# One decoder layer on one core: attention score products from float32r parts on two row halves, and a new order of the products

## The reference

```python
q = (x @ w_q.T).reshape(B, S, 16, 16); k = ...; v = ...
scores = jnp.einsum('bqhd,bkhd->bhqk', q, k) * scale      # 4 x 16 heads, each 1024 x 1024
weights = jax.nn.softmax(scores, axis=-1)
out = jnp.einsum('bhqk,bkhd->bqhd', weights, v)
```

## Time and profile before

| | |
|---|---|
| time, median of 3 runs | 1436.05 us (1436.03 to 1437.87) |
| profiled execution: span from first to last instruction | 1435.9 us |
| share of the span: PE, DVE, ACT, POOL | 98%, 75%, 60%, 39% |

### The profile page before, as it was taken

One profiled execution on the slowest core, in us unless ns is written; L12 is line 12 of the kernel. 1 busy time (PEld: TensorE's weight loads), 2 busy tenths in 40 slices (PEclk: granted clock), 3 DMA queues, 4 the chain that ended last, 5 costly groups with the idle time before them and its releaser, 6 DMA issues.

```text
span 1435.9 us, 48815 instructions
## 1 busy us (share of the span) xinstructions
PE 1400.5 (98%) x18550; PEld 933.5 (65%) x18550; DVE 1076.8 (75%) x1963; ACT 863.0 (60%) x1973; POOL 556.4 (39%) x952
## 2 busy tenths in 40 slices
PE   9999999999999999999999999999999999999995
PEld 5445455544444444444444448889889999999994
DVE  6888888888888888888999955767555655555553
ACT  4688888877777777778877783333233333333331
POOL 2221211222222222531213413677775555555554
PEclk9999999999999999999999999999999999999998
DMA  6235555444434323432422342222332222222221
GB/s 210 63 106 171 165 162 168 131 110 126 117 105 142 86 64 89 118 85 68 137 81 69 102 147 92 72 86 87 121 101 81 75 75 75 75 74 70 77 75 48
DMA packets 108799, 147.39 MB, mean 103 GB/s; under 512 B 28027, under 2 KB 80570, under 8 KB 107546
## 3 DMA queue, kind: packets, MB, share of 16 engines
q1 hardware_dynamic: 94026, 104.92, 25.6%
q0 software_dynamic: 13968, 38.05, 8.0%
q10 hardware_dynamic: 576, 1.31, 0.3%
HBM read 81.17 MB, written 63.04 MB: 100 GB/s over the span
## 4 chain that ended last, share of the span: by engine, by line
PE 81%; DVE 8%; issue 4%; POOL 3%; ACT 1%; DMA 1%; DVEq 0%; POOLq 0%; ACTq 0%
PE pa L939 15%; PE pa L1187 14%; PE pb L939 13%; PE po L1115 13%; PE pb L1201 13%; PE px L939 6%; DVE neg L1476 3%; PE px L932 2%; PE pb L932 1%; ACT w_sb L1304 1%; PE po L1046 1%; PE po L932 1%; PE px L1021 1%; PE px L993 1%; DMA space<-y_parts,y_tags 1%
## 5 line engine op out<-in xcount | busy, mean ns | idle before, releaser
L1476 DVE TENSOR_REDUCE neg<-pa 128x1 f32<-128x1024 f32 x512 | 611.4, 1213 | 76.8 <-PE pa L939 69.3
L1304 ACT ACTIVATE w_sb<-pb 128x512 f32<-128x512 f32 x996 | 590.0, 598 | 105.2 <-PE pb L939 69.7
L939 PE MATMUL pb<-w_sb 99*32 99x512 bf16 x3984 | 392.1, 380 | 3.6 <-ACT w_sb L1304 2.0
L1420 ACT ACTIVATE space<-pa,b1T_sb 128x128 f32<-128x128 f32 x568 | 154.3, 383 | 322.7 <-PE pa L1187 320.2
L939 PE MATMUL pa<-w_sb 96*32 96x512 bf16 (+1 forms) x4208 | 323.1, 380 | 6.1 <-DVE neg L1476 6.1
L1115 PE MATMUL po<-w_sb,space 128*32 128x256 f32 x4000 | 304.6, 379 | 0.0
L1187 PE MATMUL pa<-xgT,attn_t 128*128 128x128 f32 x2272 | 269.3, 276 | 2.9 <-DVE attn_t L1814 2.9
L1187 PEld LDWEIGHTS pa<-xgT,attn_t 128*128 128x128 f32 x2272 | 265.7, 192 | 8.9 <-issue 5.6
L1201 PE MATMUL pb<-w_sb,space 128*128 x1136 | 260.4, 379 | 0.0
L1201 PEld LDWEIGHTS pb<-w_sb,space 128*128 128x128 f32 x1136 | 208.8, 190 | 25.1 <-issue 0.3
L1115 PEld LDWEIGHTS po<-w_sb,space 128*32 128x32 f32 x4000 | 124.3, 111 | 98.6
(11 more groups left out here) (242 smaller groups left out, 1234.1 us busy)
## 6 DMA issues: line engine op xcount, KB each, us to landing
y_parts<-attn_t SPq DMA_DIRECT2D x13, 896.0 KB, 4.9
w_sb<-w SPq DMA_DIRECT2D x17, 512.0 KB, 4.7
attention_out<-space SPq DMA_DIRECT2D x64, 128.0 KB
w_sb<-w SPq DMA_DIRECT2D x7, 1024.0 KB, 8.0
xg<-x_by_expert SPq DMA_DIRECT2D x54, 130.0 KB, 2.1
q_parts<-w_sb SPq DMA_DIRECT2D x48, 128.0 KB, 3.1
w_sb<-q_parts SPq DMA_DIRECT2D x64, 96.0 KB, 2.6
w_sb<-k_parts SPq DMA_DIRECT2D x64, 96.0 KB, 3.0
```

The costliest lines, as they stand in the source:

```text
L939: mm = pe.matmul(out[at:end], lhsT[:, at:end], rhs, start=start, stop=stop, tile_position=(0, at))
L1304: act.activation(ex_of(n)[:, half * HALF:(half + 1) * HALF], score_bank(n, half), ACT.Exp, scale=SCALE).then_inc(e_done, 1)
L1420: ins = act.activation(hT[tile % 2][:, f, :], pH[tile % 2][:, f, :], ACT.Relu, bias=g.b1_sb[:, bass.ds(e * FT + f, 1)])
L1476: dve.tensor_reduce(neg[i % 2][:, t:t + 1], pa[n % 2][:, :], AX.X, ALU.max, negate=True).then_inc(max_done, 1)
```

## The change

- Parts: q and k are split into two float32r parts (high, low), 3 pairs of parts (high-high, low-high or high-low, twice 16 rows beside) make 48 rows, 50 with the maxima's two parts. ACT makes the high part, DVE the low part; POOL's middle and low parts are gone, and two of its four small operations for the maxima.
- Place: the stacked operands of a head lie on partitions 0 to 49 or 64 to 113, two heads on one half, two on the other (`rows_of`). A product is one instruction with 128 columns of weights and 512 moving columns, at row position 0 or 64. Exponent product and maximum product belong to heads two apart, so they are on different halves.
- Order: both halves of the exponent product and both of the maximum product of a tile are issued as a run of four, then the sums, for each of the two tiles; the side piece comes last, behind both maximum products.
- Loads: 4 transfers for a head where there were 6, of the same 384 KB in all; 2 stores of parts where there were 3.
- Around it: the first loads wait for the memory settings that fill the ones rows; four statistics tiles shrink to two slots; the last weight loads are cut by partition halves and not by column halves alone.

The core of the diff:

```diff
-STACK = 6 * HD
-FULL = STACK + 3
+STACK = 3 * HD
+FULL = STACK + 2
...
+        def rows_of(i):
+            return i // 2 % 2 * (P // 2)
...
-                def remainder(b, i):
+                def low_part(b, i):
                     which = i % 2
-                    n = nth(b, i)
-                    dve.wait_ge(h_done, n)
-                    if n > 2:
-                        dve.wait_ge(l_done, n - 2)
-                    dve.tensor_tensor(rest[:, n % 2, :], px[:, :], part[:, which, 0, :], ALU.subtract).then_inc(rest_done, 1)
+                    dve.wait_ge(h_done, nth(b, i))
+                    dve.tensor_tensor(part[:, which, 1, :].bitcast(F32R), px[:, :], part[:, which, 0, :], ALU.subtract
+                                      ).then_inc(l_done, 1)
...
-                def score_max(n):
+                def score_max(n, half):
                     i, t = divmod(n, TB)
...
+                    r = rows_of(i)
+                    rows = slice(r, r + STACK)
+                    mm = pe.matmul(pa[n % 2][:, half * HALF:(half + 1) * HALF],
+                                   q_ring[rows, i % 2, t * P:(t + 1) * P],
+                                   k_ring[rows, i % 2, half * HALF:(half + 1) * HALF], start=True, stop=True, tile_position=(r, 0))
...
                 for p in range(PAIRS):
-                    score_exp(2 * p, 0)
-                    if p:
-                        sums(2 * p - 2)
-                    score_exp(2 * p, 1)
-                    if p:
-                        sums(2 * p - 1)
-                    score_exp(2 * p + 1, 0)
-                    if p + LEAD < PAIRS:
-                        score_max(2 * (p + LEAD))
-                    score_exp(2 * p + 1, 1)
+                    for n in (2 * p, 2 * p + 1):
+                        for half in range(2):
+                            score_exp(n, half)
+                            if p + LEAD < PAIRS:
+                                score_max(n + 2 * LEAD, half)
+                        if p:
+                            sums(n - 2)
                     side(p)
-                    if p + LEAD < PAIRS:
-                        score_max(2 * (p + LEAD) + 1)
```

More of the change, by code:

```diff
@@ L6 @@
 from concourse import mybir
-F32, BF16 = mybir.dt.float32, mybir.dt.bfloat16
+F32, F32R = mybir.dt.float32, mybir.dt.float32r
 I32, U32 = mybir.dt.int32, mybir.dt.uint32
@@ L235, in stream @@
         v_all = room(8192, 4096).rearrange("p (h t d) -> p h t d", h=2 * H, t=TB)
-        part = room(12288, 1536).bitcast(BF16).rearrange("p (w a c) -> p w a c", w=2, a=3)
-        rest = room(13824, 1024).rearrange("p (n c) -> p n c", n=2)
+        part = room(12288, 2048).rearrange("p (w a c) -> p w a c", w=2, a=2)
         xs = room(14848, 1024).rearrange("p (k c) -> p k c", k=KD)
@@ L423, in load_w_qk @@
             eng.dma_start(w_qk[:, which, k], (g.wqT, g.wkT)[which][k * P:(k + 1) * P, :]).then_inc((q_in, k_in)[which][k], 16)
-        W2_LOADS = NE + 1
+        W2_LOADS = NE + 4
         halves = [slice(i * FT // 2, (i + 1) * FT // 2) for i in range(2)]
+        low, high = slice(0, P // 2), slice(P // 2, P)
         def number(eng, tile, which):
@@ L466, in store_group @@
                     c, m, which = group(b, i)
-                    dram, rows = ((q_dram, Q_ROWS), (k_dram, K_ROWS))[which]
+                    dram = (q_dram, k_dram)[which]
                     n = nth(b, i)
@@ L608, in _ @@
                 for i in range(4, GROUPS):
-                    for name in "hml":
+                    for name in PARTS:
                         store_first(i, name)
@@ L630, in _ @@
                         settle(sp, g.settled_dma)
-                        load_w2(sp, 0)
+                        for e in range(2):
+                            load_w2(sp, e, rows=low)
                         sp.wait_ge(pv_done, MOVED // 2 - 1)
@@ L642, in _ @@
                         settle(sp, g.settled_dma)
-                        load_w2(sp, 1, halves[0])
+                        for e in range(2):
+                            load_w2(sp, e, halves[0], high)
                     if i + 1 < NH:
@@ L833, in _ @@
                                            c_bv.rearrange("p (o d) -> p o d", o=1).to_broadcast([C, B, D]), ALU.add).then_inc(cv_made, 1)
-                    if s == 1 and b:
-                        lower_parts(b, turn % TB)
                     if s == 3 and j is not None:
@@ L1103, in score_exp @@
                         pe.wait_ge(e_done, 2 * n - 1 + half)
-                    quarters(score_bank(n, half), ks[i % RING][:, t * P:(t + 1) * P],
-                             qs[i % RING][:, half * HALF:(half + 1) * HALF], True, True).then_inc(b_done, 1)
+                    r = rows_of(i)
+                    rows = slice(r, r + FULL)
+                    pe.matmul(score_bank(n, half), k_ring[rows, i % 2, t * P:(t + 1) * P],
+                              q_ring[rows, i % 2, half * HALF:(half + 1) * HALF], start=True, stop=True, tile_position=(r, 0)
+                              ).then_inc(b_done, 1)
                 def sums(n):
@@ L1410, in _ @@
                 settle(act, settled_act)
-                load_w2(act, 1, halves[1])
+                for e in range(2):
+                    load_w2(act, e, halves[1], high)
                 take_output(NH - 1)
@@ L1819, in _ @@
                     dve.memset(neg_parts[i][:, :], 0.0).then_inc(set_up, 1)
-                for i in range(RING):
-                    dve.memset(ks[i][STACK:FULL, :], 1.0).then_inc(set_up, 1)
+                for r in range(0, P, P // 2):
+                    dve.memset(k_ring[r + 32:r + P // 2, :, :].bitcast(F32), 1.0).then_inc(set_up, 1)
                 dve.memset(g.run[:, :], 0.0)
```

166 lines of the change are left out of this document (67 added, 99 removed).

## The result

The changed kernel takes 1599.14 us (median of 4 runs, 1597.78 to 1603.54), the kernel before beside it 1436.61 us; the ratio is 1.1135, 95% interval 1.1119 to 1.1152. Ratios with an interval leave out those runs of a kernel that are more than 1.5% above its fastest one, which show a lower mean granted clock. The profiled execution has a span of 1596.0 us, 160.1 more than before. The forecast was 1487: right in sign, inside the range of 1438 to 1612, and 110 us too low.

A forecast was written before the change was run, and what follows sets the result against it. PE was taken to bound the attention, DVE and ACT close behind. Full turns +43, turns 0 to 8 +1 and turns 24 to 30 +6, together +50 on 1435.9, gave 1487 us; range 1438 to 1612.

The forecast's parts named there:

- the wait for the maxima: PE's second run waits for DVE's reduction: pairs behind s = 0, 2, 7 take 3.74, 3.70, 3.74 us.
- 3.33: Full turn: us added by the pairs behind s = 0, 2, 7 over three pairs of 2.616.
- the streaming of a run: PE's run of four: one step a column, both row halves at once, 0.436 us a run.
- rival (a): PE's runs: halves do not overlap or float32r takes two steps, 0.872 a run; 1606 us, chance 0.20.
- I take 0.12 for each change: PE changes between column quarters and row halves four times a pair, each costing 0.12 us, bounds 0 and 0.17.
- the loop through ACT: Next tile's second exponent half waits 1.61 us from this tile's first half; an ordinary pair takes 2.50 instead of 2.62.
- The own range given with the forecast: Whole kernel: 1465 to 1520 us, from form changes of 0.05 to 0.17 and second-half weights 0.1 late in a run.
- (b): DVE's chain before the next pair's second run is hidden, all 248 pairs gain 0.12; 1399 us, chance 0.08.
- (c): PE's changes of form cost nothing, an ordinary pair takes 2.26 us; 1439 us, chance 0.07.
- (d): PE's runs: two steps a column and no overlap, a pair takes 4.84 us; 1987 us, chance 0.04.
- costed at nothing: POOL's dropped parts, a head's loads, first loads, last turn, feed-forward part and start: no time gained or lost.
- +0.83: Late turns (24 to 30): us added a turn by longer pairs behind s = 7 and 2, x 7 = +6.

The follow-up runs named there:

- e_act: Changed kernel with ACT's copy of a head's output moved behind all four exponentials of a pair; 1.0748 times the kernel before.
- e_both: Changed kernel with both moves: DVE reduces both maxima before its side work, ACT copies the head's sums behind all four exponentials; 1.0067 times the kernel before.
- e_dve: Changed kernel with one line of DVE's order moved: both maxima of a pair are reduced before its side work; 1.0400 times the kernel before.
- after_again: The changed kernel once more, unchanged, on the third chip; 1.1188 times the kernel before.
- e_same_half: Changed kernel with exponent and maximum product of a run on the same row half, one last-weight load a head later; 1.4526 times the kernel before.
- e_parts_same: New parts and row halves in the order before, exponent and maximum product on the same row half; 1699.15 to 1782.3 us against 1435.26 for the kernel before.
- e_order: The kernel before (three bf16 parts, column quarters) with only the order of the changed one; 1.0767 times the kernel before.

## Why the prediction was right in sign and short by 110 us

**Right: the wait for the maxima.** "The pair behind s = 0, 2, 7 takes 3.74, 3.70, 3.74." Behind s = 2 it took 3.69 (498.05 to the next side piece at 501.74), behind s = 0 in the first turns 3.86, and behind s = 7 3.90 (late turns of `e_act`). Removing these waits took 3.3 us out of a full turn; in the forecast's own pairs that would have been 3.74 + 3.70 + 3.74 - 3 x 2.50 = 3.68, since it had the ordinary pair too short, and its 3.33 was counted from the pairs of before. Which pairs wait (67, where 68 were counted), and who is queued behind the waiting product, came out too.

**Right: the streaming of a run.** One step a column, both halves at once. In a run the four products take 0.34 + 0.33 with two starts; rival (a), no overlap, falls although its time, 1606, is nearest to the result. The Trainium skill, page TensorEngine Tiling (Array Packing), section Theoretical Speedup, which the forecast cites against (a), gives up to 2x for 64 rows or fewer. The trace agrees for the streaming (starts 122.83 and 122.83); for a whole tile it is 1.71 against 1.24, 1.4x.

**Too small: "I take 0.12 for each change".** It was worked out as two changes for a tile, 0.24. The trace has three delays of 0.11 to 0.13: sums to first product (0.57 less 0.44), first product to second (0.34 less 0.21), second to sums (0.33 less 0.21). PE alone would need 2 x 1.24 = 2.48 for a pair. But the wait for the bank stays, as forecast, and both parts of that sum are longer: the loop through ACT is 1.67 (122.83 to 124.50) and not 1.61, and from there to the pair's end it is 1.00 (124.50 to 125.50) and not 0.89. So the ordinary pair is 2.67, not 2.50, and the change of products alone is a small loss (`e_both` 1.0067) instead of a gain of 0.12 a pair. By turns (first ones 24.03 against 23.62 before, full ones 27.16 against 26.83, where -0.84 and -0.43 were in the sum) this is 1.25 x 9 + 0.76 x 15 + 0.2 x 7 = 24 us. The own range given with the forecast named this as a possibility, and did not suffice.

**Missed: ACT's wait for the sums.** The part on the order looked at what PE's move does to DVE and at the loop of exponentials, and not at the third reader that ACT has: `take_output`, in every fourth pair. It costs 1.14 x 9 + 0.77 x 15 + 1.7 x 7 = 34 us (in late turns from `e_dve` and `e_both`: pairs s = 0 and 4 3.73 against 2.67 and 3.04). The view that would have shown it was at hand: ACT's instructions in order, each with the product that it reads, and where that product stands now.

**Missed: the granted clock.** The forecast took the full clock as given since it stands in every slice of before. By the clock column of the windows, which is rounded, PE is at half the clock for 2 x (0.07 x 249.1 + 0.01 x 474.4 + 0.14 x 225.1) = 107 us of the attention. First turns are 249.1 - 9 x 26.26 = 13 us over the pace at full clock, full ones 474.4 - 15 x 31.2 = 6, late ones 225.1 - 7 x 30.1 = 14, and 1.5 more in most late turns, whose pair s = 1 (4.59 instead of 3.04) runs at half the clock: about 44 us, in which the slower turns also hold some waits for POOL and for transfers. The six runs of `after_again` bear the size out: they go from 1594.75 us at a mean clock of 0.964 to 1639.42 at 0.930, some 13 us for 0.01, and from 0.962, the clock of the result's trace, to the 0.996 of before that would be 45 us, an estimate.

**Right but for the last turn: the rest.** (b) falls with the 67 waits, (c) with the delays at each change, (d) with the run of 0.34 + 0.33. PE's waits name DVE and ACT alone, so POOL's parts and the head's loads, which were costed at nothing, cost nothing. But the last turn was taken to be paced by ACT, and it is PE that paces it: busy for 18.95 of 19 us before (842 to 861), for 20.0 of 20 after (997 to 1017). It takes 4.7 us more. Turn 0 starts 1.0 us later than before.

**The late turns.** +0.83 was forecast, about 5.2 measured in the best ones. Beside the two points above, both waits meet in the pair s = 0 there and add up (4.97: 3.73 with one wait, and 1.24 for the chain), where the forecast had compared with one row of before that was itself a long one (3.35; most are 3.18). Of the 5.2 the forecast's 0.83, the form (0.2), ACT's wait (1.7) and the clock (1.5) leave 1.0 a turn for the chains, 7 us.

**The balance.** 24 + 34 + 44 + 7 = 109 us. These terms are counted from the undisturbed turns of before (23.6, 26.8 and 24.9 us), over which its own stages lie by 1, 1 and 4 us; less these 6 it is 103, where the three stages grew by 153.8 - 50 = 104 more than forecast. The other 6 us of the 110 are the last turn (4.7), the later start (1.0) and a rest. The terms of waits and form come from experiments that take them away; the clock's is what is left over in the slower turns.

**The cause of the half clock stays open.** What goes with it: the same order and waits with the old products have 1.00, 1.00 and 0.98 in the stages, the new products without the waits 0.99, 1.00 and 0.97, both together 0.93, 0.99 and 0.86. One kind of wait is enough: `e_dve`, which keeps only the one through ACT, has 0.92, 1.00 and 0.91. In the result's trace each of the 15 falls ahead of the feed-forward part comes 0.3 to 2.4 us behind the end of a wait of PE, and in `e_same_half` each of the 39 within 3.0 us. But far more waits are followed by no fall, and `e_parts_same` falls at 1029.8 us without one, so no single account of what PE did before the clock fell covers all of them. The comparison of old and new products has a gap, too: `e_order` ran on the second chip alone, and the changed kernel never ran there, so that the chip keeps the clock up in `e_order` is not excluded. A filler of PE's waits was not tried.

## What to carry to other kernels

When an order changes on one engine, list every instruction on the other engines that reads or frees one of the moved results, with its place in that engine's queue, and not just the readers of the streams that seem to matter; here a copy in every fourth pair was worth 34 us. A form that halves the streaming has to be priced by the starts it exposes: 0.36 us a tile took back most of the 0.44 that the shorter products save. The little that was left went into the bank: with one bank for each half a tile's second exponent product starts no sooner than 1.67 us behind the first one of the tile before, so that an ordinary pair takes 2.67 where PE's own pace of 1.24 a tile would make 2.48. Nothing was won even with the two moves; a second pair of banks was not tried. Such a reordering wants its companions moved too: with DVE's and ACT's two moves the same order cost 0.4% with the old products and 0.7% with the new ones, instead of 7.7 and 11%; none of the versions beat the kernel before.

## What was not expected of the hardware

A float32r product streams 512 columns in at most 0.24 us (the later ones of `e_same_half` follow each other at 0.24, and at 0.43 at half the clock), as fast as a bf16 one (0.22), but the first one behind a change of form holds the next back to 0.34 us. A late load of its 128 columns of weights would explain it, and is not shown by itself. Changing between column quarters and row halves costs 0.34 to 0.36 us for in and out together; the Trainium skill, page TensorEngine Tiling (Array Packing), section Key Properties, says that a change of mode drains the engine; the trace agrees that the change costs, with this number.

The granted clock can fall from 2.4 to 1.2 GHz while PE is busy all the time: in `e_parts_same` it was 1.00 until 1029.7 us and 0.50 behind it, with PE busy 49.7 of 49.7 us and 102.2 of 102.2. In the runs with the new products in the changed order, ahead of the feed-forward part, it fell within 3.0 us behind the end of a wait of PE of 0.3 to 1.7 us. And a kernel that kept the clock throughout its attention can lose it by a change of the order and the form of its products.
